# Spreading the low half's inverse sums ahead of the routing-table stores on GpSimd

## What is computed

```
def xattn(q, k, v):                       # q [16,128,512]; k = v = ctx [16,128,512]
    qh, kh, vh = (t.reshape(16 * 8, 16, 512) for t in (q, k, v))
    qk = einsum('bdm,bdn->bmn', qh, kh) / sqrt(16)
    return einsum('bmn,bcn->bcm', softmax(qk), vh).reshape(16, 128, 512)

def ffn(x, wg, W, b):                     # 2048 tokens of 512, 8 experts
    probs = softmax(xt @ wg); idx = argmax(probs); gate = probs[idx]
    return gate * (xt @ W[idx].T + b[idx])

x = x + tanh(g_xattn) * xattn(layernorm(x), ctx, ctx)
x = x + tanh(g_ffn)   * ffn(layernorm(x), wg, W, b)
```

## Time and profile before

| | us |
|---|---|
| median of 3 runs | 643.95 |
| the 3 runs | 641.86, 643.95, 647.44 |
| the profiled execution | 647.44 |
| its span, first to last instruction | 645.8 |

### The profile page before, as it was taken

How to read it: one execution, slowest core, us unless ns; L and a number is a source line. 1 busy time by engine, 2 the same in 40 slices (tenths; PEclk the granted TensorE clock), 3 DMA queues, 4 the chain that set the end, 5 groups by cost and what they waited for, 6 DMA issues and landing times. The chain is left out here.

```text
span 645.8 us, 9542 instructions
## 1 busy us (share of the span) xinstructions
PE 533.5 (83%) x2556; PEld 180.7 (28%) x2603; DVE 448.2 (69%) x883; ACT 350.1 (54%) x429; POOL 370.6 (57%) x631
## 2 busy tenths in 40 slices
PE   0077999998989899899999999798599689289993
PEld 0011222322323232232323223232222145144551
DVE  5487789888888888888998888789686634101110
ACT  2111777776787777678777767766367621011110
POOL 5432648767585856758586776866243734414441
PEclk9999999999999999999999999999989899779997
DMA  4754365766658576674645557574730344323410
GB/s 134 187 151 160 73 179 124 198 157 180 180 168 220 126 213 154 180 182 106 181 122 128 160 128 133 133 96 125 27 121 5 88 149 140 101 89 116 127 59 0
DMA packets 35046, 85.52 MB, mean 132 GB/s; under 512 B 10233, under 2 KB 10365, under 8 KB 34977
## 3 DMA queue, kind: packets, MB, share of 16 engines
q1 hardware_dynamic: 22848, 59.46, 39.5%
q0 software_dynamic: 12160, 25.62, 12.0%
HBM read 62.56 MB, written 27.15 MB: 139 GB/s over the span
## 5 line engine op out<-in xcount | busy, mean ns | idle before, releaser
L801 DVE TENSOR_REDUCE neg_max<-ps_ring 128x1 f32<-128x512 f32 x512 | 332.0, 681 | 62.4 <-PE ps_ring L1129 54.0
L726 ACT ACTIVATE probs<-ps_scores 128x1024 f32<-128x1024 f32 x256 | 251.6, 1023 | 97.5 <-PE ps_scores L1147 80.8
L1129 PE MATMUL ps_ring<-stacks 96*128 96x512 bf16 x512 | 199.4, 403 | 64.7 <-DMA stacks<-parts_dram 30.6
L1147 PE MATMUL ps_scores<-stacks 128*128 128x512 bf16 x471 | 146.4, 387 | 12.8 <-ACT probs L726 5.4
L1166 PE MATMUL ps_pv<-probs,v_ones 128*32 128x512 f32 x1024 | 139.0, 615 | 0.4 <-issue 0.4
L1129 PEld LDWEIGHTS ps_ring<-stacks 96*128 96x128 bf16 x512 | 49.5, 97 | 259.8 <-DVE neg_max L801 207.4
L1223 PE MATMUL ps_scores<-w_sb,f_xt 128*128 x184 | 84.9, 605 | 1.2 <-ACT f_xt L719 0.9
L1147 PEld LDWEIGHTS ps_scores<-stacks 128*128 128x128 bf16 x512 | 47.9, 101 | 55.6 <-ACT probs L726 19.4
L519 POOL DMA_DIRECT2D stacks<-shift_parts x96 | 50.0, 523 | 20.3 <-POOL shift_parts L512 17.5
L444 POOL TENSOR_SCALAR rs<-mv 128x1 f32<-128x1 f32 x32 | 6.0, 187 | 95.7 <-DVE mv L817 45.4
L719 ACT COPY f_xt<-ps_scores 128x512 f32<-128x512 f32 x23 | 13.4, 587 | 86.6 <-PE ps_scores L1206 86.6
(11 more groups left out here) (139 smaller groups left out, 474.9 us busy)
## 6 DMA issues: line engine op xcount, KB each, us to landing
parts_dram<-prep POOLq DMA_DIRECT2D x16, 768.0 KB
stacks<-parts_dram SPq DMA_DIRECT2D x64, 192.0 KB
stacks<-parts_dram SPq DMA_DIRECT2D x64, 128.0 KB
w_sb<-w_t SPq DMA_DIRECT2D x16, 512.0 KB, 8.7
recs_dram<-rec SPq DMA_DIRECT2D x16, 512.0 KB, 11.6
prep<-x_perm SPq DMA_DIRECT2D x16, 256.0 KB, 5.1
prep<-k_perm SPq DMA_DIRECT2D x16, 256.0 KB, 8.7
v_in<-v_t SPq DMA_DIRECT2D x16, 256.0 KB, 10.1
```

The source lines that it names most:

```text
L726: nc.scalar.activation(probs[:, k % 2, 2 * jp:2 * jp + 2], ps_scores[:, jp], ACT.Exp).then_inc(exp_done, 1)
L801: nc.vector.tensor_reduce(neg_max[:, g, j, c:c + 1], ps_ring[:, u.slot(n)], AX.X, ALU.max, negate=True).then_inc(ring_free, 1)
L1129: nc.tensor.matmul(ps_ring[:, u.slot(n + c)], q_stack[0:KS, B.p, g, j, c * 128:(c + 1) * 128], k_stack[0:KS, B.p, g, j], start=True, stop= ...
L1147: last = nc.tensor.matmul(ps_scores[:, jp, j % 2], k_stack[0:KA, B.p, g, j, c * 128:(c + 1) * 128], q_stack[0:KA, B.p, g, j], start=True, ...
```

## The change

In `emit` of GpSimd, the call that spreads the inverse sums of group 0 of batch B is moved from behind the table stores to ahead of them. Nothing is added or taken away. The two orders differ only in batches that store tokens at this place: batches 9, 10, 11, 12 (two stores each) and 13 (four stores). The three waits that stand with the stores (for `table_set` and `dest_ready`) now stand behind the spread too.

```diff
@@ -623,6 +623,7 @@
                     lows(B.plus(3))
                 if nxt:
                     copy_values(B.plus(1))
+                spread_sums(B, 0)
                 if B.known(ROUTED[0]):
                     pool.wait_ge(table_set, 16)
                     pool.wait_ge(dest_ready, 1)
@@ -631,7 +632,6 @@
                 if B.known(ROUTED[1]):
                     pool.wait_ge(dest_ready, 2)
                     store_tokens(*GROUPS[1])
-                spread_sums(B, 0)
                 if B.known(ROUTED[1] + 1):
                     read_slots(0)
                     records_stored(GROUPS[1][1])
```

## The result

The changed kernel takes 651.47 us (median of four runs, 650.95 to 657.06) where the kernel before took 645.56 us in the same measurement. The ratio is 1.0107, with a 95% interval of 1.0066 to 1.0148. Timed again later on another chip it was 648.28 against 642.78 us, ratio 1.0084 (1.0053 to 1.0116). So the moved line costs close to 6 us. The profiled execution took 653.81 us, its span is 652.2.

What follows compares the result with a forecast made beforehand. No engine was full (TensorE nearest, 83%); TensorE and VectorE carried the chain, GpSimd 1%. Batches 9 to 11 at 0, batch 12 at 0 to 0.1 and batch 13 at 0 on the 643.95 us median gave 644.0 us, range 639.5 to 649.

Steps and rivals of the forecast that it cites:

- The views and the part of GpSimd: Busy times, last-ending chain, GpSimd's timeline and shift-load landings; GpSimd, 1% of the chain, matters only through what others wait for.
- The gain of the early spread: VectorE's turning back, batches 9 to 11: zero, since its 0.79 us wait is for group 1's spread; at most 2.4 us.
- Batches 9 to 11: 0: Stores end 1.8 us later on GpSimd, 2.9 us of its idle time are left, nothing behind them moves; cost 0.
- Batch 12: GpSimd's two stores end at 428.6, its next work starts at 428.62; cover used up within 0.1 us, cost 0 to 0.1.
- Batch 13: Four stores move behind the spread, batch 14's split and shift load 3.3 us later; taken as 0, bounds 0 and +6.1.
- the stop: 5.33 us from 462.60 with nothing released in the chain; taken as about the profiled execution's 5.6 us distance to the fastest.
- Rival 1: Slower: batch 14's shift load lands late and TensorE's step 4 scores wait; 647.5 us, 653 at worst; chance 0.16.
- Rival 2: Faster: slow transfers from 455 are the stores' wake, so the stop vanishes; up to -8.2 us, likelier 638.7; chance 0.08.
- Rival 3: VectorE's turning back really gains from the early spread; at most 2.4 us, 641.6 us; chance 0.02.
- The rule on the strongly ordered increment: Batch 14's shift load not reported before the last store lands, 471.3: in time for 473.4, 0.7 us late for 470.6.
- The low clock: TensorE, after standing still for batch 14's shift load, runs at the low clock for up to 2.9 us more.

Runs made afterwards that it cites:

- e4: No table stores in batches 9 to 13, all twelve at the end of batch 14 ahead of the table's read; ratio 1.0317 to the kernel before.
- g8_new_order: The changed order with table rows of 32 bytes per entry; 636.44 us against 642.78 for the kernel before, ratio 0.9893.
- e1: Spread moved ahead of the stores in batches 9 to 12 only, batch 13 in the old order; 652.55 against 644.82 us before, ratio 1.0121.
- e2: Spread moved ahead of the stores in batch 13 only; 647.27 us, ratio 1.0042 to the kernel before.
- e5: Stores put in mid-batch, behind the shift load of group 0 and ahead of the low parts' store; ratio 1.0111 to the kernel before.
- e8a: Like e4, plus twelve stores to an unread second table in the changed kernel's place, to the same neighbouring rows; ratio 1.0452 to the kernel before.
- e8b: Like e8a, but the second table's entries go to rows 512 bytes apart; ratio 1.0350 to the kernel before.

## Why the prediction was wrong, step by step

- **The views and the part of GpSimd** were read rightly: its own times moved as worked out, in all five batches; in batch 13 the split of batch 14 starts 3.4 us later than VectorE's copy allows (3.3 were forecast). The gain of the early spread was zero, as forecast: VectorE's turning back waits as before (2.4 us in 3 cases from 330 to 500 us in both).
- **"Batches 9 to 11: 0", the failed step.** The working said that nothing behind the stores moves, since 2.9 us of GpSimd's idle time are left. That covers GpSimd, not the transfers: the path from the stores over the DMA to the landing of the shift load was put at nothing. The stores' own transfers go on for 2.4 us each, as e4 measured, and each pair is issued later than before, nearer to the shift load. By that rate alone (an estimate) batch 9's pair would have landed at 344.3, 4 us before the shift load is issued; how the delay gets from one to the other is not shown. That the stores cause it is: with rows of their own in the same order the load of batch 10 lands in 1.9 to 2.2 us (g8_new_order) instead of 4.4 to 6.9, and no score waits. TensorE waited 1.76, 1.82, 0.69 and 1.43 us in batches 10 to 13, and its low clock came on top behind the first two. e1 has 1.2% for these batches alone. Batch 12 ("0 to 0.1") fails by the same step. The trace of before held the sign: batch 10's quick landing was taken for all, but batch 12's load, behind batch 11's stores, took 6.1/6.5/7.3 us, and that is the wait of 2.1 us in the earlier trace rows.
- **Batch 13** was bounded rightly (0 to +6.1) and taken wrongly (0). I argued that an execution without the stop would be without slow landings. e2 has no stop, and its load of batch 14 lands in 8.2 to 11.5 us. Nor does the stop mark the slow executions, as the working had it from 5.33 against 5.6 us: e1's fastest has it too. The runs show that both are one thing, a wake of the stores (slow transfers for some us behind them) that falls where the stores are put: the stop is in the traces of before, e1 and e5 (whose batch 13 has no low parts, so that its stores stand practically in the old place), and in no trace where batch 13's stores come later or have rows of their own. Moved behind the spread, the wake missed the stop and met the shift load: 5.40 us in the changed kernel, 6.32 in e2.
- **Rival 1** had the right wait and too small a scope, one batch instead of five. **Rival 2** had the right mechanism with the wrong sign of the sum; its own objection, that the wake would fall on the shift load and be given back, is what happened. **Rival 3** didn't occur.
- **The rule on the strongly ordered increment** (the Trainium skill, "DMA: Bandwidth & Descriptors", queues, rings and completion order) was weighed for batch 13 only, and there set aside. The traces agree with what it says, that a completion waits for earlier writes of its engine: the shift loads' landings go up to 8.4 us when slow writes stand ahead (e8a) and to 5.9 when the same number of writes to rows apart does (e8b). They don't show whether it is the increment or the data that is held up.
- **The low clock** was counted in the rival only. In the changed kernel it followed the waits of batches 10, 11 and 14, and the passage to the experts had 0.60 over 17 us against 0.80 before. What it cost in all was not separated.

Left open: what exactly stood still in the stop of 5.3 us. TensorE's matmuls stand in the record up to 463.4, and ScalarE and VectorE, which read their results, go on at 467.9; from 462 to 467 the transfers moved 40 GB/s. A load of code held up by the same wake would fit, but no run here separates it. Nor do the 2.4 us of a store account for the length of the slow stretch behind four stores (32 GB/s on the mean from 455 to 468 us), and it wasn't tried whether the loads that share the stretch are held up in HBM or in the DMA engines.

## What to carry to other kernels

An instruction that issues a transfer is over long before the transfer is: when such an instruction is moved, lay its landing, not its issue, beside what others wait for, and count how many small writes go into the same few bytes. A scatter of 8-byte entries to neighbouring rows took 2.4 us for 128 of them and slowed the transfers behind it; rows of 32 bytes each made the kernel 0.6 and 1.2% faster on two chips and took the price of the order from 5.5 to 1.4 us. If slow transfers are seen behind one kind of store in the profile of before, treat them as its wake and ask what the wake will meet in the new place.

## What was not expected of the hardware

- Writes of 8 bytes side by side are slow: twelve stores of 128 such writes landed in 28.7 us, with 32 bytes to each in 18.1 us, of which 15.1 are GpSimd's issuing.
- The loss shows in the wait of another transfer, not in the stores' own record: the issue takes about 1 us on GpSimd in every run, quick or slow.
- The length of a wait alone does not tell whether TensorE's granted clock falls. Around waits of 1.76 and 1.82 us it was 0.81 and 0.88 over 5 us in the changed kernel, but around the wait of 2.14 us in batch 12 of the kernel before it stayed at 1.00 (411 to 418 us).
